# A vision-transformer layer on one core: where waits, row loads, table arithmetic and idle-time multiplications stand

## The reference, cut to what matters

```python
h = layernorm(patchify(x) @ W) * gamma            # 16 images, 256 tokens each, 320 -> 256 features
y = layernorm(h)
q, k, v, g = silu(y@Wq), silu(y@Wk), y@Wv, sigmoid(y@Wg)      # 16 heads of 64
decay = exp(where(causal, cum_i - cum_j, -inf)), cum = cumsum(-softplus(y@Wa + ba))
o = ((q k^T) * decay) @ v                         # no softmax
h = h + (groupnorm_per_head(o) * g) @ Wo
y = layernorm(h)
top-2 of 8 experts by softmax(y @ w_router)
h = h + sum over the two of weight * (gelu(y @ w1[e] + b1[e]) @ w2[e] + b2[e])    # 256 -> 1024 -> 256
```

## Time and profile before

| | us |
|---|---|
| median of 3 runs | 1288.66 |
| lowest and highest | 1285.53, 1288.92 |
| the profiled execution, its own time | 1284.18 |
| its span in the trace | 1282.3 |

### The profile page before, as it was taken

The page is one execution under the profiler, slowest core; times in us unless marked ns, Lnnn a source line. Parts: engine busy times, 40 slices in busy tenths (PEclk is TensorE's granted clock), DMA queues, the critical chain, the costliest instruction groups (busy, mean ns, idle before and its releaser), DMA issues. The chain is left out here.

```text
span 1282.3 us, 27300 instructions
## 1 busy us (share of the span) xinstructions
PE 1243.4 (97%) x8534; PEld 1068.5 (83%) x8534; DVE 824.9 (64%) x2120; ACT 858.1 (67%) x2019; POOL 426.6 (33%) x524
## 2 busy tenths in 40 slices
PE   6999999999999999999999999999999999999996
PEld 5777788788787877877877777889999999999995
DVE  5455565666666667666566566557788888565561
ACT  4767666667658557567567566447788888666672
POOL 2211121242151241141241151354354454433433
PEclk8999999999999999999999999999999999999998
DMA  5532222233233233232232237288988887989883
GB/s 189 168 101 84 92 88 91 85 113 107 81 115 109 78 117 109 69 126 92 78 123 68 94 118 241 91 239 248 259 230 246 220 225 190 276 264 269 253 238 82
DMA packets 125607, 194.46 MB, mean 152 GB/s; under 512 B 16272, under 2 KB 91504, under 8 KB 125360
## 3 DMA queue, kind: packets, MB, share of 16 engines
q1 hardware_dynamic: 110864, 175.37, 43.1%
q0 software_dynamic: 13584, 17.26, 6.6%
q10 hardware_dynamic: 1056, 0.55, 0.2%
HBM read 167.40 MB, written 29.05 MB: 153 GB/s over the span
## 5 line engine op out<-in xcount | busy, mean ns | idle before, releaser
L1193 PE MATMUL bank<-xn_sp,big_r 128*128 128x512 f32 x1152 | 312.0, 408 | 1.0 <-DVE xn_sp L1692 1.0
L1193 PEld LDWEIGHTS bank<-xn_sp,big_r 128*128 128x128 f32 x1152 | 204.4, 188 | 54.2 <-issue 1.7
L1720 DVE TENSOR_TENSOR att<-bank,dec_x 128x384 f32<-128x384 f32 x256 | 130.5, 551 | 100.6 <-PE bank L1232 95.2
L838 ACT ACTIVATE dec_x<-dec_x,ncum 128x256 f32<-128x256 f32 (+1 forms) x512 | 189.8, 445 | 6.7 <-POOL dec_x L665 6.7
L665 POOL TENSOR_SCALAR_AFFINE_SELECT dec_x<-dec_x 128x256 f32<-128x256 f32 x256 | 108.1, 450 | 226.7 <-DMA dec_x<-cum_scratch 226.2
L1538 PE MATMUL bank<-big_r 128*128 128x256 f32 x1296 | 169.1, 287 | 2.2 <-ACT mid_f L908 2.2
L1538 PEld LDWEIGHTS bank<-big_r 128*128 128x128 f32 x1296 | 162.0, 193 | 3.3 <-ACT mid_f L908 2.4
L716 POOL TENSOR_SCALAR mid_f<-mid_f,dec_x 128x256 f32<-128x256 f32 x71 | 76.3, 1080 | 185.1 <-DVE mid_f L1971 180.0
L1987 DVE TENSOR_TENSOR big_r<-mid_f,big_r 128x256 fp32r<-128x256 f32 x216 | 91.3, 423 | 70.8 <-ACT big_r L928 70.8
L722 POOL DMA_INDIRECT out<-mid_f,tok x71 | 118.8, 1673 | 51.9 <-POOL mid_f L716 21.0
L908 ACT ACTIVATE mid_f<-bank,h 128x256 f32<-128x256 f32 x216 | 101.3, 478 | 42.3 <-PE bank L1538 20.2
(11 more groups left out here) (230 smaller groups left out, 2216.2 us busy)
## 6 DMA issues: line engine op xcount, KB each, us to landing
big_f<-in_L_ffn_w SPq DMA_DIRECT2D x68, 1024.0 KB, 7.9
dec_x<-cum_scratch SPq DMA_DIRECT2D x128, 384.0 KB, 3.7
big_w<-in_L_ffn_w SPq DMA_DIRECT2D x12, 1024.0 KB, 6.2
mid_f<-expert_rows SPq DMA_DIRECT2D x27, 261.0 KB, 3.2
h_scratch<-h SPq DMA_DIRECT2D x16, 256.0 KB, 2.3
h<-h_scratch SPq DMA_DIRECT2D x8, 512.0 KB, 4.2
out<-h SPq DMA_DIRECT2D x16, 256.0 KB, 4.1
xt<-in_x SPq DMA_DIRECT2D x15, 256.0 KB, 3.9
```

What stands on the lines that cost most here:

```text
L838: act.activation(d, d, ACT.Exp, bias=ncum[p % 2][:, NS * u + s, 2 * c + hh:2 * c + hh + 1]).then_inc(M["exp_done"], 1)
L1193: mm = pe.matmul(bank[target][:, :], wp[:, k, c * P:(c + 1) * P], xp[:, k, :], start=(k == 0 and j == 0), stop=(k == EC - 1 and j == 2))
L1720: dve.tensor_tensor(att[hh][:, :], bank[4 + hh][:, 0:LW], dec[n % RING][:, hh, :], ALU.mult).then_inc(M["mult_done"], 1)
```

## The change

Seven edits. (1) b1 and b2 of a block get semaphores of their own; the first gelu waits for b1 only, and `keep_y` waits for b2. (2) In `load_pair` the rows of the next m are issued ahead of the unit's w2 and the next m's w2; its b1 stays where the rows were. With it, `row_tails` in `mixed_row` goes from c == 4 to c == 0 (before `hidden_lo` of chunk 1 and before `keep_y`). (3) `first_tables` goes from step 0 to step 2 of pair 7, and a copy of the counts is taken at the old place. (4) In pair 6 `route` of an image goes from the end of step 6 into step 7; in pair 7 DVE does `decayed` of the second image ahead of `head_stats` and `y_lo`. (5) At the end of the pairs PE takes `turn2` and `route` of the last two images two or more pieces later, and ACT does gelus 4 to 7 of block 1 ahead of the second `keep_x2`. (6) In the prologue PE multiplies zeros in three places, five times each; DVE clears the tile for it first. (7) `tokens(2)` goes from the prologue into step 0 of pair 0.

```diff
+        cnt1 = room(242, X)
...
             def load_b1(e, par):
-                ... .then_inc(M[f"b_in{par}"], 16)
+                ... .then_inc(M[f"b1_in{par}"], 16)
...
             def load_pair(one, nxt, after, parity):
-                load_one(one)
+                e_one = unit_rows_and_layer1(one)
+                e_nxt = rows_only(nxt)
+                unit_layer2(one, e_one)
                 weights2_ahead(nxt)
                 bias2(one)
-                rows_whole(nxt)
+                bias1(nxt, e_nxt)
...
             def active(k, c, target, width):
                 if c == 0:
-                    act.wait_ge(M[f"b_in{k.par}"], 32 * (k.n + 1))
+                    act.wait_ge(M[f"b1_in{k.par}"], 16 * (k.n + 1))
...
             keep_x2(2 * NPR - 2)
-            active_early(1, 4)
+            for c in range(4, HC):
+                active_early(1, c)
             keep_x2(2 * NPR - 1)
-            for c in range(5, HC):
-                active_early(1, c)
...
+            def keep_running(n):
+                for i in range(n):
+                    pe.matmul(bank[5][:, 0:E], att[0][:, 0:P], att[0][:, P:P + E], start=True, stop=True)
+            pe.wait_ge(M["cleared"], 1)
+            keep_running(5)
             pe.wait_ge(M["wt_in"], 32)
...
                 if pair(p + 2):
                     tokens(2 * p + 4)
+                elif pair(p - 1):
+                    route(2 * p - 1)
...
+                    if p == 0 and c == 0:
+                        tokens(2)
...
-                if c == 6 and post:
+                if c == 6 and post and p != NPR - 2:
                     route(2 * p - 1)
...
             tokens(1)
+            keep_running(5)
             turn(0)
-            tokens(2)
+            keep_running(5)
             turn(1)
...
-            early2(0, 4)
-            early2(0, 5)
+            for c in range(4, HC):
+                early2(0, c)
             turn2(2 * NPR - 2, "h2_done", 2 * NPR)
-            early2(0, 6)
-            early2(0, 7)
+            early1(1, 4)
+            early1(1, 5)
             route(2 * NPR - 2)
-            early1(1, 4)
-            turn2(2 * NPR - 1, "lg_done", 2 * NPR - 1)
-            early1(1, 5)
-            route(2 * NPR - 1)
             early1(1, 6)
             early1(1, 7)
+            turn2(2 * NPR - 1, "lg_done", 2 * NPR - 1)
             turn_early(2)
             early2(1, 0)
+            route(2 * NPR - 1)
...
             def keep_y(k, pieces):
                 dve.wait_ge(M["y_ps"], k.j + 1)
+                dve.wait_ge(M[f"b2_in{k.par}"], 16 * (k.n + 1))
...
                 if main:
+                    if p == NPR - 1:
+                        decayed(p, 7, 1)
                     head_stats(p, 6)
                     y_lo(p, 0, 0)
-                    decayed(p, 7, 1)
+                    if p < NPR - 1:
+                        decayed(p, 7, 1)
...
                 if c == 0:
                     if p == NPR - 1:
-                        first_tables()
+                        first_counts()
...
                 if c == 2:
+                    if p == NPR - 1:
+                        first_tables()
...
+            dve.memset(att[0][:, :], 0.0).then_inc(M["cleared"], 1)
...
             def mixed_row(k, b_par, before, pieces, last):
                     if c == 2:
                         keep_y(before, pieces)
-                    if c == 4:
+                    if c == 0:
                         row_tails(k, rows_f[0], BS)
```

More of the change, by code:

```diff
@@ L291, in vit_layer @@
         names = """
-        passed mh_done zeroed c_in c_sum ws_in0 ws_in1 ws_in2 ws_in3 ws_hi ws_lo wt_in g_in
+        cleared passed mh_done zeroed c_in c_sum ws_in0 ws_in1 ws_in2 ws_in3 ws_hi ws_lo wt_in g_in
         xt_in xt_in1 tok_ps s1_st s1_u s1_v0 s1_v1 s1_st2 s1_ve s1_rs s1_h s1_xn
@@ L300, in vit_layer @@
         tope_done trec_done wall_done idxf_done pick_done both_done rk_ps rank_done taken_done rsel_done
-        slot_done tail_done scat0 scat1 scat2 scat3 late_out tb1_in tb_in wf_in0 wf_in1 wf_in2 wf_in3 w1_inx tb1
+        slot_done tail_done scat0 scat1 scat2 scat3 late_out tb1_in cnt1_done tb_in wf_in0 wf_in1 wf_in2 wf_in3 w1_inx tb1
         tb pad_out
-        row_in0 row_in1 w1_in0 w1_in1 w2_in0 w2_in1 b_in0 b_in1 xe_ps xe_hi xe_lo w1_hi w1_lo w2_hi w2_lo
+        row_in0 row_in1 w1_in0 w1_in1 w2_in0 w2_in1 b1_in0 b1_in1 b2_in0 b2_in1 xe_ps xe_hi xe_lo w1_hi w1_lo w2_hi w2_lo
         hid_ps gel_done gh_done gl_done y_half y_ps y_done ecol_done wk_done wsel_done y_w added
@@ L410, in load_b1 @@
             def load_b1(e, par):
-                sp.dma_start(b1_sb[par], b1[bass.ds(e, 1), :, :].rearrange("a p k -> (a p) k")).then_inc(M[f"b_in{par}"], 16)
+                sp.dma_start(b1_sb[par], b1[bass.ds(e, 1), :, :].rearrange("a p k -> (a p) k")).then_inc(M[f"b1_in{par}"], 16)
             def load_b2(e, par):
-                sp.dma_start(b2_sb[par], b2[bass.ds(e, 1), :].broadcast_to([P, E])).then_inc(M[f"b_in{par}"], 16)
+                sp.dma_start(b2_sb[par], b2[bass.ds(e, 1), :].broadcast_to([P, E])).then_inc(M[f"b2_in{par}"], 16)
             def load_rows(r, par):
@@ L534, in weights_whole, with rows_only @@
                 load_w2(e, w2_f[k.par], f"w2_in{k.par}")
-            def rows_whole(k):
+            def rows_only(k):
                 e, r = expert(k.j), place(k.j)
@@ L543, in rows_whole, with bias1 @@
                 load_rows(r, k.par)
+                return e
+            def bias1(k, e):
                 sp.wait_ge(M["gel_done"], HC * (k.j - 1))
                 load_b1(e, k.par)
+            def rows_whole(k):
+                bias1(k, rows_only(k))
             def bias2(k):
@@ L568, in weights2_ahead, with unit_rows_and_layer1 @@
                 load_w2(e, w2_f[0], "w2_in0")
-            def load_one(k):
+            def unit_rows_and_layer1(k):
                 e, r = expert(k.j), place(k.j)
@@ L579, in load_one, with unit_layer2 @@
                 load_b1(e, 1)
+                return e
+            def unit_layer2(k, e):
                 sp.wait_ge(M["w2_lo"], WQ * NL)
@@ L582, in load_one @@
                 load_w2(e, w2_f[1], "w2_in1")
+            def load_one(k):
+                unit_layer2(k, unit_rows_and_layer1(k))
             def load_pair(one, nxt, after, parity):
-                load_one(one)
+                e_one = unit_rows_and_layer1(one)
+                e_nxt = rows_only(nxt)
+                unit_layer2(one, e_one)
                 weights2_ahead(nxt)
                 bias2(one)
-                rows_whole(nxt)
+                bias1(nxt, e_nxt)
                 if after is not None:
@@ L1877, in along, with first_counts @@
                 return x.rearrange("p (a n) -> p a n", a=1).broadcast_to([P, n, X])
+            def first_counts():
+                dve.wait_ge(M["taken_done"], EARLY)
+                dve.wait_ge(M["h_out"], 16 * B)
+                dve.tensor_copy(cnt1, cnt).then_inc(M["cnt1_done"], 1)
             def first_tables():
                 dve.wait_ge(M["tb1_in"], 16)
-                dve.wait_ge(M["taken_done"], EARLY)
-                dve.wait_ge(M["h_out"], 16 * B)
+                dve.wait_ge(M["cnt1_done"], 1)
                 cut = cut1.rearrange("p (n a) -> p n a", a=N1)
                 cmp1 = cut1.rearrange("p (a n) -> p a n", a=N1)
-                t1(dve.tensor_tensor(cut, cnt.rearrange("p (n a) -> p n a", a=1).broadcast_to([P, X, N1]), iob1, ALU.is_ge))
+                t1(dve.tensor_tensor(cut, cnt1.rearrange("p (n a) -> p n a", a=1).broadcast_to([P, X, N1]), iob1, ALU.is_ge))
                 t1(dve.tensor_reduce(nb1, cut, AX.X, ALU.add))
@@ L2199, in earlier @@
             def earlier(k):
-                return k._replace(j=k.j - 1, par=1 - k.par, r1=k.r1 - 2)
+                return k._replace(j=k.j - 1, par=1 - k.par, n=k.n - 1, r1=k.r1 - 2)
             with dve.Fori(NF // 2, LAST // 2 - 1) as q:
```

## The result

The changed kernel takes 1299.77 us (median of 5, 1298.57 to 1302.11), where the kernel before takes 1288.92 (median of 5, 1285.53 to 1291.85). The ratio is 1.0086, 95% interval 1.0064 to 1.0109: slower by 11 us, outside the range that I gave.

What follows compares the result with a forecast made beforehand. PE was taken as the bound, busy 1243.4 of 1282.3 us. The terms summed to +0.95 us, which on the median of 1288.66 gave 1289.6; the forecast's own range was 1285.5 to 1293.5, with rivals 1277 to 1297.

Steps and rivals of the forecast that it cites:

- prologue: Start of the kernel: moving tokens(2) into step 0 costs 1.0 us, the zeros give 0; ends -2.1 and +1.
- tables: Pair 7: a wait of PE in step 1 goes, -1.85 us, step 2 loses 0.3; net -1.55.
- route, decayed: Pairs 6 and 7: nothing at 699; the 0.74 us stall at 796 moves to the group norm; +0.05 us.
- turns: Turns of the last images, 826 and 832: PE's waits mostly go, net -1.8 us, ends -2.3 and 0.
- bias semaphores: Block 6, near 900: ACT's gelu stops waiting for b2, but weights land late; gain 2.9 us, 3.8 with no wait.
- mixed rounds: Rounds after 1098: earlier rows give -5.45 us, PE's pauses before layer 2 cost 11.6.
- Rival C: Prologue: zeros keep the clock up until the work of 25, sum 2.1 lower, 1287.5 us; chance 0.46 together with the forecast.
- the wait for `added`: Mixed rounds: row_tails at c == 0 waits for scatters, holding PE before layer 2 1.45 us a round, +11.6 over eight.
- Y + 12.85: Mixed rounds: forecast start of layer 2, Y being the end of the layer 2 before; Y + 11.4 without stalls.
- rival D: Mixed rounds: a late unit scatter holds the next tails and the x split beyond 2 us of room; 1297.6; 0.22 with another rival.
- The gain of the rows: Mixed rounds: rows issued some 4 us earlier are there in time, -5.45 us over eight rounds; ends 4.3 and 5.45.
- rival A: Mixed rounds: the wait for `added` costs nothing, as scatters land before Y + 9.3; sum -10.65, 1278.0 us; chance 0.32.

Runs made afterwards that it cites:

- the four runs above: Four places again, without zeros, with tokens(2) back in the prologue, and with both: 1274.05, 1274.64, 1274.55 and 1275.24 us.
- four places: The changed kernel with four places instead of two for token numbers and weights (tok, wsel) in the mixed rounds: 1274.10 us, ratio 0.9896.
- the old order back: Four places with tables, route, decayed and the last images' turns and gelus at their old places, the counts' copy kept: 1280.11 us, ratio 0.9924.
- the mixed edit alone: The kernel before with only the early rows and row_tails at c == 0: 1308.18 us, ratio 1.0153.
- the mixed edit undone: The changed kernel with loads in the old order and row_tails back at c == 4: 1279.92 us, ratio 0.9940.

## Why the prediction was wrong, by its own steps

| step | predicted | by the two traces |
|---|---|---|
| prologue | +1.0 | +2.06 (second scores 44.34, 46.40) |
| tables | -1.55 | -1.54 (-2.19 at 733, +0.65 at 754) |
| route, decayed | +0.05 | +0.04 |
| turns | -1.8 | -1.97 at 839, 0.73 lost at 854 |
| bias semaphores | -2.9 | -4.19 |
| mixed rounds | +6.15 | +19.28, and 0.85 behind them |
| sum | +0.95 | +15.3 |

The right column compares one execution of each kernel, so it holds their spread too. Of the prologue's +2.06 the four runs above show nothing in the time, and starts of one prologue differ by 2.85 us. One step in it was wrong on the zeros: I put each group at 1.2 us and the first one's end at about 3.7; by the trace they take 4.63, 2.32 and 2.32, and the first ends at 5.9. Rival C didn't come. The granted clock of the changed kernel is 0.50 from 22 to 34 us, so the fall came earlier, as I had written beside it.

**What held.** The mechanism of the largest term: PE stands before layer 2, since `row_tails` waits for the second scatter with `keep_y` queued behind it; with four places that is gone, which shows it. The tables came to -1.54 for -1.55, but the closeness is luck: the parts were -2.19 for -1.85 and +0.65 for +0.3. The stall of 796 does move to the group norm, at 799:

```profile
753.13 0.80 PE L1268 MATMUL bank<-att,mid_f 128*64 128x256 f32 x3 [0.22 <-DVE att L1748]
...
799.71 0.36 PE L1280 MATMUL bank<-gst,half 128*128 128x8 f32 x2 [0.78 <-DVE gst L1752]
...
854.63 3.72 PE L1364 MATMUL bank<-xs,big_w 128*128 128x256 f32 x16 [0.46 <-ACT xs L900]
```

The 0.46 at 854 isn't the turns': with the old order back PE waits 1.08 there, and 0.87 in the run of the mixed edit alone, which has the old order too. The trace of before, with none, is the exception.

**The step that failed is the price of the wait for `added`.** I put it at 8 x 1.45 = 11.6, the length of eight pauses and nothing else. Against stall-free rounds of 19.16, the eight rounds take 178.01 - 153.28 = 24.7. This comes apart as follows.

- The pauses before layer 2 in the eight rounds are 3.16, 1.89, 0.92, 1.59, 1.93, 1.58, 1.61 and 0.70: 13.4. My 11.6 stood for the eight rounds that follow another one, and these are the second to the ninth. Their pauses are 11.1 in all (the ninth's, 0.84, is what the table has behind the rounds), so this part was right. The first round I had left out, and its 3.16 is the longest pause. Within the 11.1 two errors meet. I had Y + 12.85 for the start of layer 2 and the mean is Y + 13.5, since the landings took longer than the 4.75 that I used (from the second scatter's issue at 1179.33 to the tails at 1185.62 are 6.3). But the turn ahead of it came later too, in the rounds that had lost time before it.
- The x split waits in three rounds, 2.2 in all (L2017 above). That is rival D, which I gave 2 us of room.
```profile
1097.00:1099.00 2.00, 2.00 (x10) 2.00 (x11) 2.00 (x5) 2.00 (x7) 1.98 (x2) 0.50 0.90 259
...
1188.00:1190.00 2.00, 2.00 (x12) 2.00 (x12) 1.82 (x4) 2.00 (x7) 1.14 (x2) 0.53 0.90 280
```

**The bias term was mis-sized by a row of two loads.** I had the weights land at 900.8, from a row that gives one figure for w1 and w2 together (10.6). In the changed kernel they were issued at 889.16 and 889.65; ACT went through their first piece at 897.45 without a wait, and layer 1 of block 6 ran at 899.21 in 3.04 us, with no pause. The true limit of that term was my "no wait", 3.8, and 4.19 came. It holds the fall of the clock behind that stall in before, which not every execution has. That the semaphores do more is shown by putting them back: 9.4 us, of which 4.2 in the mixed rounds by the traces. My "they'd be what is late next once the rows come early" was right, and in the sum it should have made the rows' gain depend on this edit.

**The gain of the rows, -5.45, was right, but under a condition.** It came whole (rounds of 19.17) once the wait was free; that is rival A's world, at 1274 and not 1278. Of the rest, 1.3 is in the bias term. My step from one execution to a median, 4.5 us added, also took the spread as the same in both kernels. It isn't: the changed kernel's profiled execution is its median, 1299.77.

**What stays open.** Why the scatters land later in the changed kernel: from the second one's issue to the tails, 6.8, 6.5 and 6.3 us in three of the four rounds from 1113, where six of the eight of before took under 5. Its trace has no landing times for them. The load beside them may be part of it. In the 5 us from the issue the mean busy share of the DMA engines is 0.98, 1.02 and 0.89 in these three and 0.75 and 0.81 in the two quickest (4.2 and 4.4 us). But before has 0.94 beside a landing of 4.1. And what decides whether the clock falls behind a pause: the same pauses of before have it in one execution and not in another.

## What to carry to other kernels

Price a wait on the bottleneck engine as its length plus what follows it: here 13.4 us of pauses cost 24.7, with a second stall, three falls of the clock and 2.4 us that I take for the refill. When a call with a wait is moved up in an in-order queue, look for what it now stands in front of; here one place further down, or two more places in two small tables, turned a loss of 11 us into a gain of 8 or of 13 to 16. And undo each half of a paired edit before dropping the pair. One half was tried here, the other (early `row_tails`, loads in the old order) was not: rows ahead of weights cost 12 us with `row_tails` late, and gave all they promised with it early and free.

## What the runs showed that I had not expected

The clock's falls are no function of the pause ahead of them alone. In the mixed rounds no pause of up to 1.61 us had one behind it. Those of 1.89, 1.93 and 3.16 in the changed kernel did (granted 0.50 and near it), as did 1.94 with the tables back, 2.17 in the earlier trace rows, 2.45 with row_tails at c == 4, and five of 2.51 to 3.33 with the mixed edit alone. But 1.85 with row_tails at c == 4, 1.82 and 1.95 with the mixed edit alone and 2.55 with one bias semaphore had none: behind the last, 18 multiplications took the usual 2.53 us. And in pair 6 a fall stands behind less: two pauses of 1.11 and 0.42 us in the run with the mixed edit undone, and of 1.12 and 0.27 in the run with no zeros and tokens(2) back. The same step of four places, with pauses of 1.12 and 0.48, has none. Here are the six multiplications behind the second pause and the stretch of the fall with the mixed edit undone, then the same six in four places:

```profile
703.02 2.90 PE L1216 MATMUL bank<-xn_sp,big_r 128*128 128x512 f32 x6 [0.42 <-DVE xn_sp L1718]
```

```profile
702.00:704.00 2.00, 1.58 (x10) 1.16 (x7) 2.00 (x3) 1.60 (x2) 0.00 (x0) 0.59 0.44 124
```

```profile
701.41 1.65 PE L1221 MATMUL bank<-xn_sp,big_r 128*128 128x512 f32 x6 [0.48 <-DVE xn_sp L1723]
```

And a prologue that does the same work in the same order reached the second scores between 43.55 and 46.40 us in eight executions: an edit there worth less than 2 us can't be read from one pair of traces.
